# Sigmoid and silu written with Exp and Tanh in a transformer layer with a mixture of experts

## The reference

```python
logits = xf @ gate_w.T
scores = jax.nn.sigmoid(logits)
sfc = scores + gate_bias
...
masked = jnp.where(emask > 0, sfc, -jnp.inf)
_, topk_idx = jax.lax.top_k(masked, K)
topk_w = jnp.take_along_axis(scores, topk_idx, axis=1)
...
act = jax.nn.silu(hg) * hu
y = jnp.einsum('nei,ne,ehi->nh', act, cw, Wd)
shared = jax.nn.silu(xf @ Ws_g.T) * (xf @ Ws_u.T) @ Ws_d.T
y = y + shared
```

## Time and profile before

| what | value |
|---|---|
| median of 3 runs | 1130.15 us (1129.67 to 1133.27) |
| the profiled execution | 1136.02 us |
| its span | 1134.2 us |
| mean granted TensorE clock | 0.844 of full speed |
| TensorE (PE) matmuls | 886.7 us busy, 78% of the span |
| VectorE (DVE) | 679.0 us, 60% |
| ScalarE (ACT) | 448.6 us, 40% |
| GpSimd (POOL) | 440.0 us, 39% |

### The profile page before, as it was taken

How to read it: one execution, slowest core, us unless ns; L and a number is a source line. 1 busy time by engine, 2 the same in 40 slices (tenths; PEclk the granted TensorE clock), 3 DMA queues, 4 the chain that set the end, 5 groups by cost and what they waited for, 6 DMA issues and landing times.

```text
span 1134.2 us, 21559 instructions
## 1 busy us (share of the span) xinstructions
PE 886.7 (78%) x7044; PEld 651.4 (57%) x7044; DVE 679.0 (60%) x1918; ACT 448.6 (40%) x756; POOL 440.0 (39%) x422
## 2 busy tenths in 40 slices
PE   4369798887987997888886798695987699988810
PEld 3245465664654665655564555584875588877700
DVE  4467658677668578577476475552652233677737
ACT  2115444444343444443442445342542355444400
POOL 4422113125316316306313114454555545555642
PEclk9659898897798698798696789898998999988955
DMA  3684716217226235324465322343544555987764
GB/s 131 149 228 106 215 39 168 67 36 216 73 53 176 85 76 163 103 76 115 118 228 178 106 73 93 112 149 105 158 138 159 169 164 166 362 303 260 243 243 149
DMA packets 101467, 168.78 MB, mean 149 GB/s; under 512 B 14704, under 2 KB 73072, under 8 KB 101104
## 3 DMA queue, kind: packets, MB, share of 16 engines
q1 hardware_dynamic: 87536, 128.85, 39.7%
q0 software_dynamic: 13824, 38.55, 9.0%
HBM read 90.15 MB, written 76.68 MB: 147 GB/s over the span
## 4 chain that ended last, share of the span: by engine, by line
PE 46%; DVE 17%; issue 11%; SPq 8%; DMA 7%; ACT 6%; POOL 3%; another core or an unknown queue 2%; ACTq 0%; DVEq 0%; POOLq 0%
PE ring L1444 6%; PE ring L1316 6%; PE ring L1250 5%; PE ring L1251 4%; PE ring L1252 4%; PE ring L1287 4%; PE ring L1302 4%; ACT prob L1180 3%; DVE nmax L778 3%; DMA xg<-sorted_rows 3%; PE ring L1465 3%; SPq L581 2%; PE ring L1264 2%; PE ring L1430 2%
## 5 line engine op out<-in xcount | busy, mean ns | idle before, releaser
L778 DVE TENSOR_REDUCE nmax<-ring 128x2 f32<-128x1024 f32 (+3 forms) x256 | 201.2, 818 | 103.8 <-PE ring L1293 87.3
L1180 ACT ACTIVATE prob<-ring 128x1024 f32<-128x1024 f32 (+1 forms) x192 | 164.1, 879 | 217.4 <-PE ring L1307 195.8
L688 POOL DMA_INDIRECT expert_rows<-ys,dest x160 | 157.1, 982 | 139.3 <-ACT ys L1134 80.5
L680 POOL DMA_INDIRECT sorted_rows<-xr,idx_all x128 | 127.5, 996 | 86.9 <-DVE xr L937 53.7
L1444 PE MATMUL ring<-we,xh 128*128 x640 | 159.8, 395 | 0.0
L1287 PE MATMUL ring<-k_st,q_st 48*128 48x512 f32 (+3 forms) x512 | 116.0, 460 | 42.4 <-ACT prob L1180 35.6
L1302 PE MATMUL ring<-q_st,k_st 50*128 50x384 f32 (+3 forms) x512 | 109.3, 445 | 34.0 <-DMA q_st<-mrow 10.8
L1444 PEld LDWEIGHTS ring<-we,xh 128*128 128x128 f32 x640 | 121.6, 200 | 14.4
L1000 DVE SCALAR_TENSOR_TENSOR sl<-sl,got,ring 128x128 f32<-128x128 f32 x160 | 48.4, 344 | 123.1 <-ACT sl L1232 88.3
L1316 PE MATMUL ring<-prob,v_sb 128*32 128x512 f32 (+3 forms) x1024 | 111.6, 539 | 0.8 <-ACT prob L1180 0.4
L658 POOL TENSOR_TENSOR rot<-rot 128x512 f32<-128x512 f32 x16 | 20.4, 1273 | 222.5 <-DVE rot L770 222.5
(11 more groups left out here) (192 smaller groups left out, 1672.3 us busy)
## 6 DMA issues: line engine op xcount, KB each, us to landing
xg<-sorted_rows SPq DMA_DIRECT2D x160, 134.0 KB
parts<-part SPq DMA_DIRECT2D x32, 512.0 KB
ykt<-expert_rows SPq DMA_DIRECT2D x16, 1024.0 KB
k_st<-parts SPq DMA_DIRECT2D x64, 128.0 KB
q_st<-parts SPq DMA_DIRECT2D x64, 128.0 KB
we<-w_exp SPq DMA_DIRECT2D x1, 6144.0 KB, 20.0
sorted_rows<-zeros SPq DMA_DIRECT2D x2, 2144.0 KB, 10.5
sorted_rows<-zeros SPq DMA_DIRECT2D x32, 134.0 KB
```

What stands on the lines that cost most here:

```text
L680: pool.indirect_dma_start(out=xs[group_of(s)], out_offset=bass.IndirectOffsetOnAxis(ap=idx_all[:, s, t, k:k + 1], axis=0), in_=xr[:, s % 2 ...
L688: pool.indirect_dma_start(out=yk, out_offset=bass.IndirectOffsetOnAxis(ap=dest[:, j % 8, b:b + 1], axis=0), in_=ys[:, j % NYS, b, :], in_o ...
L778: dve.tensor_reduce(nmax[:, Q % 2, :, pp, qb], slot[:, :, col:col + (qb + 1) * P], AX.X, ALU.max, negate=True).then_inc(s_max, 1)
L1180: act_e.activation(prob[:, u % 2, 2 * half:2 * half + 2, 0:width], slot[:, :, 0:width], ACT.Exp, scale=SCALE).then_inc(s_exp, 1)
```

## The change

The router's sigmoid becomes 1 / (1 + exp(-x)): ScalarE takes Exp of -x, and VectorE adds 1 and takes the reciprocal, two more steps of `route`. The shared expert's silu(g) * u becomes (tanh(g/2) + 1) * g * 0.5 * u: ScalarE takes Tanh of g/2, and VectorE makes two fused operations, tied by a new semaphore, where it made one product. The experts' own Silu (line 1232) stays.

```diff
-ROUTE_STEPS = 30
+ROUTE_STEPS = 32
...
+        s_gate = sem("shared_gates")
...
                 dve.wait_ge(s_score, s + 1)
+                step(dve.tensor_scalar(r_sc[:, :], r_sc[:, :], 1.0, None, ALU.add))
+                step(dve.reciprocal(r_sc[:, :], r_sc[:, :]))
                 step(dve.tensor_tensor(r_sf[:, :], r_sc[:, :], kc[:, K_BIAS:K_BIAS + NT * E], ALU.add))
...
                     dve.wait_ge(s_gu, 4 * n + 2 * u + 2)
                     if n:
                         dve.wait_ge(s_alo, 2 * n - 1 + u)
-                    dve.tensor_tensor(act[:, u, :], silu[:, u, :], ring[RING_SLOT[st]][:, 1, :], ALU.mult).then_inc(s_t, 1)
+                    gate, up = ring[RING_SLOT[st]][:, 0, :], ring[RING_SLOT[st]][:, 1, :]
+                    dve.scalar_tensor_tensor(silu[:, u, :], silu[:, u, :], 1.0, gate, ALU.add, ALU.mult).then_inc(s_gate, 1)
+                    dve.wait_ge(s_gate, 2 * n + u + 1)
+                    dve.scalar_tensor_tensor(act[:, u, :], silu[:, u, :], 0.5, up, ALU.mult, ALU.mult).then_inc(s_t, 1)
...
-                    act_e.activation(r_sc[:, :], r_lg[:, :], ACT.Sigmoid).then_inc(s_score, 1)
+                    act_e.activation(r_sc[:, :], r_lg[:, :], ACT.Exp, scale=-1.0).then_inc(s_score, 1)
...
-                    act_e.activation(silu[:, u, :], slot[:, 0, :], ACT.Silu).then_inc(s_silu, 1)
+                    act_e.activation(silu[:, u, :], slot[:, 0, :], ACT.Tanh, scale=0.5).then_inc(s_silu, 1)
```

## The result

The changed kernel takes 1.0054 times as long as the kernel before, with a 95% interval of 1.0030 to 1.0078 (20 runs of each). On 1130.15 us that is +6.1 us (+3.4 to +8.8), or 1136.3 us: slower, with the lower end of the interval at 0.3%. Its runs scatter more (1128.98 to 1154.17) than those of the kernel before (1126.57 to 1141.04), and the medians of all runs lie 10.4 us apart (1140.56 and 1130.16); the ratio leaves two disturbed runs out, which alone brings the median to 1139.0 only, so the size of the loss is less sure than that there is one. The profiled execution took 1144.04 us with a span of 1141.8 us, at a mean granted clock of 0.851 (before 0.844).

What follows compares the result with a forecast made beforehand. TensorE and VectorE were taken to bound the kernel, ScalarE only where they wait for it. Shifts of 0.16 + 3.60 + 0.69 - 0.46 - 1.28 + 0.82 = +3.5 us on 1130.15 gave 1133.6 us, range 1124.5 to 1141.

Steps and rivals of the forecast that it cites:

- What bounds it: Whole kernel: ScalarE savings count only where TensorE or VectorE waits; `act` lies in the chain, 4 us before the load.
- The loads: Sigmoid, Silu, Exp trios at places 0 to 6: all go; first two worth nothing, Exp's up to 1.28 us.
- my formula with no delay: Second half of `prob`: shifts by the greater of d - 1.28 and d - idle + 0.17 + 0.03, VectorE delay d zero.
- VectorE, shared expert: At `act`: two fused operations of 740 ns replace one 688 ns product, +0.82 us a unit, delaying `mrow` and the logits.
- VectorE, router: After the scores: addition 195 ns, reciprocal 0.55 us, +0.8 us a sequence, covered by TensorE's product with `v_sb`.
- The places: Sequences 0 to 6, and sequence 7: shifts +0.16, +1.20 three times, +0.69, -0.46, -1.28 and +0.82 us.
- my own case: Whole kernel: the delays and spared loads sum to +3.5 us, 1130 to 1137; chance 0.45.
- the clock falls earlier: During the logits: longer idle time lowers TensorE's clock, +1.6 us at up to six places, 1143; chance 0.20.
- still for `mrow`: Before the logits: sign of being right, TensorE idle 2.4 us at places 0 to 3, 1.7 at 4 and 5.
- `prob` right behind `a_hi`: Behind the logits: sign of being right, `prob` following `a_hi` with no Exp load between; load worth up to 1.28 us.
- A time from logits to shared-down product that moves with the clock: Logits to shared-down product: sign of being wrong, time following the granted clock instead of the forecast shifts; no size given.
- the clock comes back earlier: Logits to shared-down product: removed stalls let the clock rise sooner, 2.2 us less at five places, 1122.6; chance 0.15.

Runs made afterwards that it cites:

- one product with 4 loads: The changed kernel with one product instead of the two fused operations, part of the computation left out: ratio 0.9994 (0.9966 to 1.0022).
- the router alone: The changed kernel with the shared expert's Silu and one product restored, only the router's part kept: ratio 0.9989 (0.9969 to 1.0008).
- the shared expert alone: The changed kernel with the router's Sigmoid restored, only Tanh and the two fused operations kept: ratio 1.0063 (1.0028 to 1.0098).
- `mrow` ahead: `mrow` put ahead of the second unit of `act`, places 0 to 5: changed kernel 0.9963, kernel before 0.9955, the router alone 0.9943.
- late router pieces: The changed kernel with the router's 12 pieces placed behind the step that makes `z`: ratio 1.0159 (1.0111 to 1.0207).

## Why the prediction was nearly right, point by point

The forecast was 1133.6 us, +3.5; measured are +6.1 (+3.4 to +8.8), inside the range of 1124.5 to 1141 and on the side that had the highest chance.

- **What bounds it**: right. `act` and `mrow` lie ahead of the logits, and with `mrow` moved out from behind the pair the changed kernel is no slower than the kernel before in the same order, within 0.5%.
- **The loads**: the count is right (21 gone) and so is the statement that two of each trio are worth nothing, since one product with 4 loads and the router alone with 18 give the same within their intervals. The worth of the third was overstated. By the step "the Exp load is worth up to 1.28 us of `prob`'s start" and my formula with no delay the router alone should gain 3 x 1.28 + 3 x 0.24 + 0.13 = 4.7 us; it gained 1.2 (at most 3.5). The changed kernel against the shared expert alone says the same (1.0054 against 1.0063, 1.0 us), and so does the pair of runs with `mrow` ahead (0.9943 against 0.9955, 1.3 us). None of the three differences is clear of nothing.
- **VectorE, shared expert**: I took 740 ns by a slope through a shorter fused operation; it is 688, the lower bound. With it the delays are 1.24 and 0.72 us where I had 1.44 and 0.82. TensorE's idle time before the logits came to 2.12 and 1.64 us (+1.20 and +0.72), where I forecast 2.4 and 1.7. In sequence 7 it waits 1.57 us for `act` instead of 0.84, +0.73 where I had +0.82.
- **VectorE, router**: 187 and 553 ns where I took 195 and 550. Covered, as forecast: the router alone doesn't lose.
- **The places**: with 688 ns the same formulas give -0.04, +1.00 three times, +0.59, -0.56, -1.28 and +0.72, together +2.4 us.
- **The term that was missing** in my own case, as far as the rows show one, is the stretch of the logits, 3.2 us. I had it as the rival *the clock falls earlier*, at +1.6 us for up to six places and with 0.20; it came at four, with +0.2, +0.7, +0.9 and +1.4 us. I had read the six places as one question with one answer, though they had two idle times (2.4 and 1.7 us) in my own list. Own case and this part of the rival make 2.4 + 3.2 = 5.6 us, beside the 6.1 measured.

That the sum comes so close is in part luck. The same working gives the shared expert alone 4 x 1.24 + 3 x 0.72 + 3.5 = 10.6 us, measured 7.1 (3.2 to 11.1), and the router alone -4.7, measured -1.2: too much loss in the one and too much gain in the other, by 3.5 us each. What the attention takes back of a shift, and where, is seen in one place only: the waits for `z`. The router alone won 6.1 us of waits for `prob` behind the logits and waited 6.3 us more for `z`. Whether the wait for `z` would stay if VectorE had less to do there is open: moving the router only moved the queue, and an order with a shorter one wasn't tried.

Of the signs that I named, *four loads left*, *still for `mrow`* and *`prob` right behind `a_hi`* were there (295.42 and 0.61 us for `a_hi`, then 296.20 at place 1, 0.17 us late for its scores). *A time from logits to shared-down product that moves with the clock* was there as well. Place 2 of the changed kernel, with its stretch at half clock, took 14.24 us at 0.53 and place 5 9.95 us at 0.83:

```profile
384.76:399.00 14.24, 14.24 (x116) 9.57 (x117) 8.87 (x23) 4.54 (x7) 7.50 (x7) 0.53 0.23 79
...
652.13:662.08 9.95, 9.89 (x117) 6.48 (x117) 6.39 (x17) 4.43 (x7) 5.47 (x5) 0.83 0.37 96
```

Over the seven places such stretches differ from the kernel before by -3.8 to +1.4 us, more than my shifts of -1.3 to +1.2. Added up over places 0 to 5 they became shorter: 72.9 us against 80.7. 5.0 us of that are waits for `prob` that are gone, and TensorE is busy 71.7 us against 75.6 with the same matmuls, although the logits among them are 3.2 us longer. So over these stretches the clock gave back more than it took, as the rival *the clock comes back earlier* had it: the mean granted clock is higher at places 0, 1, 4 and 5 (0.71, 0.72, 0.70, 0.83 where it was 0.66, 0.58, 0.57, 0.64) and lower at places 2 and 3. The sums over the six stretches, kernel before and changed kernel:

```profile
sum 80.65, PE 75.61 PEld 48.36 DVE 47.91 ACT 38.35 POOL 38.56; mean PE 12.60 PEld 8.06 DVE 7.98 ACT 6.39 POOL 6.43
...
sum 72.86, PE 71.72 PEld 48.14 DVE 43.80 ACT 27.13 POOL 33.80; mean PE 11.95 PEld 8.02 DVE 7.30 ACT 4.52 POOL 5.63
```

The time was lost elsewhere: in the waits before the logits (6.2 us more over the six places) and between the shared-down product and the next such wait (433.3 us against 420.8). The largest part of the latter is one stretch, from place 5 to place 6, at a lower clock (kernel before, then changed kernel):

```profile
660.33:708.19 47.86, 41.28 (x451) 28.07 (x450) 31.01 (x97) 25.25 (x36) 14.02 (x13) 0.96 0.20 70
...
662.08:718.87 56.79, 48.00 (x452) 31.15 (x451) 32.97 (x99) 24.16 (x35) 15.96 (x15) 0.82 0.20 69
```

With the shared expert alone, which has the same pair, this stretch took 47.6 us, so the pair by itself doesn't make it; what does is open. That is why the runs, and not this trace, carry the verdict, and why the 3.2 us of the logits can't be called the missing part of the total.

## What to carry to other kernels

Before an operation is made longer on an in-order engine, look at what stands behind it and who waits for that: here a step of 0.27 us that TensorE waits for stood behind the doubled operation, and putting it ahead took about as much off the time as the doubling had cost, or more, and was worth something in the kernel before too. Count an engine's table loads by their places, not by their number: with all 21 gone and the pair left out the time was 0.7 us less (3.8 less to 2.5 more), for 25.8 us of ScalarE. And when a forecast lengthens an idle time of TensorE, price the matmuls right behind it at the lower clock for each place by its own idle time, not for all places together.

## What the runs showed of the hardware that I had not expected

- A fused operation with two tensor operands (one in PSUM, one in SBUF, 512 columns of fp32) costs what a plain product does, 688 ns against 688, though 128 columns of it take 344. A slope taken from another form overshot by 52 ns.
- TensorE's clock fell within the 16 logits matmuls behind 2.1 us of idle time (2.06 to 3.50 us for them over the kernels with the pair). Behind 0.7 us it stayed at 1.00 during them, behind 0.9 us it stayed or fell only at their end (at most 2.05 us, at 0.93, place 2 of the kernel before). Behind 1.6 us it is mixed: 2.00 us at place 5 of all of these, and at place 4 2.00 in the changed kernel, 2.25 with the shared expert alone and 2.34 with late router pieces. Timeline of TensorE at place 3 of the changed kernel: the same matmul takes 0.26 us and then 0.37.

```profile
470.54 0.28 PE L1333 MATMUL ring<-w_gate,h_lo 128*128 128x32 f32 x1 [2.12 <-DVE mrow L1076]
470.68 0.26 PE L1334 MATMUL ring<-w_gate,h_hi 128*128 128x32 f32 x1
470.79 0.32 PE L1333 MATMUL ring<-w_gate,h_lo 128*128 128x32 f32 x1
470.94 0.38 PE L1334 MATMUL ring<-w_gate,h_hi 128*128 128x32 f32 x1
471.16 0.37 PE L1333 MATMUL ring<-w_gate,h_lo 128*128 128x32 f32 x1
```

- An activation function can share a table with others unseen in the source: Tanh stands beside Exp without a load, and behind the experts' Silu as well, while Silu and Exp need a load between them.
- The kernel before gained 0.45% (0.13 to 0.77) from `mrow` ahead, some 5 us, of which the wait before the logits explains 1.5 (5.5 to 4.0 us). The rest wasn't traced to a place.
